# Decoder layer on one Trainium2 core: skip term and half of the causal convolution computed by TensorE with 32x32 diagonal blocks, and a new order of the side jobs

## The reference

```python
xn = norm_w * (x / rms)
xi, z = split(xn @ in_proj_w.T)                 # 1024 channels each
xc = silu(causal depthwise conv of 4 taps (xi) + conv_b)
dt, Bm, Cm = split(xc @ x_proj_w.T)             # 32, 16, 16
delta = softplus(dt @ dt_proj_w.T + dt_proj_b)
h[t] = exp(delta * A) * h[t-1] + delta * Bm * xc   # 1024 channels x 16 states
y = sum over states (h * Cm) + xc * Dp          # the last product is the skip term
out = x + (y * silu(z)) @ out_proj_w.T
```

## Time and profile before

| what | value |
|---|---|
| median of 3 runs | 2717.98 us (2713.64 to 2721.95) |
| the profiled execution: its time, its span | 2722.75 us, 2720.9 us |
| scan part (first to last scan) | 66.7 to 1973.2 us |
| steady stretch used below, 12 steps (rows 2 to 13) | 292.4 to 1745.8 us |
| experts | 2036 us to the end |

### The profile page before, as it was taken

One profiled execution on the slowest core, in us unless ns is written; L12 is line 12 of the kernel. 1 busy time (PEld: TensorE's weight loads), 2 busy tenths in 40 slices (PEclk: granted clock), 3 DMA queues, 4 the chain that ended last, 5 costly groups with the idle time before them and its releaser, 6 DMA issues.

```text
span 2720.9 us, 34850 instructions
## 1 busy us (share of the span) xinstructions
PE 2318.1 (85%) x12057; PEld 1902.7 (70%) x12057; DVE 2074.4 (76%) x2272; ACT 1779.4 (65%) x4075; POOL 1686.9 (62%) x996
## 2 busy tenths in 40 slices
PE   6778889888888888888888888887669999999997
PEld 6666666666666666766656666675539999999996
DVE  4999898899899899889999988988924454445443
ACT  5668787877778787877888887777743333333331
POOL 1988888889798888879798887979810100000100
PEclk9889998999899899989999998988879999999999
DMA  6050212212020211202020220202042432433320
GB/s 204 8 168 24 82 32 65 75 28 85 12 88 15 82 53 51 85 12 85 18 82 29 75 82 15 78 11 82 13 164 87 141 121 102 142 128 118 122 102 19
DMA packets 90876, 203.02 MB, mean 75 GB/s; under 512 B 7948, under 2 KB 16794, under 8 KB 90702
## 3 DMA queue, kind: packets, MB, share of 16 engines
q1 hardware_dynamic: 81486, 179.21, 20.3%
q0 software_dynamic: 5120, 14.21, 1.6%
q10 hardware_dynamic: 4096, 7.34, 0.9%
HBM read 171.32 MB, written 29.95 MB: 74 GB/s over the span
## 4 chain that ended last, share of the span: by engine, by line
PE 32%; DVE 30%; ACT 19%; issue 11%; POOL 5%; DMA 2%; SPq 0%; ACTq 0%; DVEq 0%; POOLq 0%
DVE ring L1267 15%; PE work L1633 12%; PE ring L1633 11%; ACT ring L831 9%; DVE arena L1276 5%; DVE arena L1110 4%; DVE arena L1267 3%; PE y L1613 3%; POOL arena L982 2%; PE work L1411 1%; POOL arena L987 1%; ACT arena L678 1%; DMA arena<-bc_rows 1%; ACT arena L553 1%; ACT arena L684 1%
## 5 line engine op out<-in xcount | busy, mean ns | idle before, releaser
L982 POOL TENSOR_TENSOR arena<-arena 128x896 f32<-128x896 f32 x512 | 1057.7, 2087 | 156.8 <-PE y L1613 148.4
L1267 DVE TENSOR_TENSOR_SCAN ring<-ring,arena 128x896 f32<-128x896 f32 x384 | 776.5, 2022 | 163.9 <-ACT ring L831 139.6
L831 ACT ACTIVATE ring<-arena,small 128x224 f32<-128x224 f32 x2048 | 793.6, 437 | 132.3 <-DVE arena L1276 124.2
L1613 PE MATMUL y<-cst_sb,arena 128*112 128x128 f32 x4096 | 556.5, 287 | 164.8 <-DVE arena L1276 124.2
L1613 PEld LDWEIGHTS y<-cst_sb,arena 128*112 128x112 f32 x4096 | 483.1, 140 | 255.0 <-DVE arena L1276 161.1
L1400 PE MATMUL work<-arena 128*128 128x224 f32 x2000 | 462.0, 389 | 36.5 <-DVE arena L1110 21.8
L1400 PEld LDWEIGHTS work<-arena 128*128 128x128 f32 x2000 | 415.2, 214 | 62.5 <-DVE arena L1110 26.3
L999 POOL DMA_INDIRECT out<-res,ids x32 | 44.7, 1395 | 642.0 <-DVE mst L1324 558.8
L1276 DVE TENSOR_TENSOR arena<-ring,arena 128x896 f32<-128x896 f32 x384 | 416.0, 1083 | 6.1 <-issue 0.2
L1339 DVE SCALAR_TENSOR_TENSOR hidden_lo<-work,hidden_hi 128x448 fp32r<-128x448 f32 x128 | 80.0, 625 | 344.9 <-ACT hidden_hi L881 344.9
L987 POOL TENSOR_TENSOR arena<-arena 128x896 f32<-128x896 f32 x128 | 266.6, 2083 | 96.8 <-DVE arena L1267 96.8
(11 more groups left out here) (210 smaller groups left out, 3352.0 us busy)
## 6 DMA issues: line engine op xcount, KB each, us to landing
weights<-in_w SPq DMA_DIRECT2D x64, 1024.0 KB, 7.2
arena<-bc_rows SPq DMA_DIRECT2D x128, 448.0 KB, 4.4
arena<-in_ctx SPq DMA_DIRECT2D x16, 896.0 KB, 5.8
expert_rows<-x2e SPq DMA_DIRECT2D x1, 7224.0 KB, 29.6
xrow<-expert_rows SPq DMA_DIRECT2D x8, 903.0 KB, 11.6
arena<-in_xT SPq DMA_DIRECT2D x16, 448.0 KB, 6.7
arena<-in_x SPq DMA_DIRECT2D x16, 448.0 KB, 3.6
out<-arena ACTq DMA_DIRECT2D x32, 224.0 KB, 2.3
```

What stands on the lines that cost most here:

```text
L831: last = nc.scalar.activation(decays[s % 2][:, i * L:(i + 1) * L], delta[:, k, :], ACT.Exp, scale=a_neg[:, n:n + 1])
L982: nc.gpsimd.tensor_tensor(u[:, u_of(b, s)], dx[:, k:k + 1, :].to_broadcast([P, QN, L]), bc[:, 0, q * QN:(q + 1) * QN, :], ALU.mult).then_i ...
L1267: nc.vector.tensor_tensor_scan(states, h, u_flat[:, u_of(b, s), :], 0.0, ALU.mult, ALU.add).then_inc(scan_done, 1)
L1613: last = nc.tensor.matmul(yt_bank[0:H, o:o + P], u[:, u_of(b, s), i, h * H:(h + 1) * H], ident, is_transpose=True, start=(s % (2 * Q) == 0 ...
```

## The change

- Two small tables of weights are made once at the start by POOL, 20 instructions of 32 partitions x 256 columns: `skip_w` and `taps_w` hold, for every 32 channels, a 32x32 diagonal block of Dp or of a convolution tap.
- The skip term is added by PE: `turn_back` issues per group four 32x32 matmuls (one per 32 channels, each on its own 32 partitions of input and output) ahead of the transposes. `skip_columns` is gone, and with it `y_bank`; the backs are now ordinary jobs of a work bank. There are three work banks in place of two (`job_bank` 0 to 2).
- The pairs 1 and 2 (`TURNED`) are convolved by PE: ACT copies the projection out in one instruction, PE does 2 groups x 4 taps x 4 blocks = 32 small matmuls in a job cv1 or cv2 (`convolve`), shifted by the tap, and ACT writes the result back with the bias (`convolved`, 2 instructions). DVE convolves pairs 0 and 3 as before.
- All due slots are new.

The diff, cut:

```diff
-        job_bank, h_bank, t_bank = wb + yb, wb, yb
+        job_bank, h_bank, t_bank = wb + [yb[1], yb[0]], wb, yb
...
-        PE_AT = {"xi0.0": 0, "xi0.1": 0.01, "xi1.0": 0.02, "xi1.1": 1, "xi2.0": 1.01, "xi2.1": 1.02, "tx0": 4, "tx1": 4.01,
-                 "rt": 4.02, "xi3.0": 4.03, "xi3.1": 4.04, "out0.0": 6, "out0.1": 7, "out0.2": 7.01, "out0.3": 7.02,
-                 "out1.0": 7.03, "out1.1": 7.04, "out1.2": 9, "out1.3": 9.01, "xp": 10, "dt0": 11, "t0": 12, "dt1": 14,
-                 "rank": 14.01, "z0.0": 15, "z0.1": 15.01, "z1.0": 15.02, "plug": 17, "z1.1": 20, "z2.0": 20.01,
-                 "z2.1": 20.02, "t1": 20.03, "dt2": 21, "z3.0": 23, "z3.1": 23.01, "dt3": 25, "ssq": 26, "xatt0.0": 27,
-                 "back0": 8.5, "back1": 16.5, "back2": 24.5, "back3": 0.5,
-                 "xatt0.1": 27.01, "xatt0.2": 27.02, "xatt1.0": 27.03, "xatt1.1": 32, "xatt1.2": 32.01}
+        PE_AT = {"xi0.0": 0, "xi0.1": 0.01, "xi1.0": 0.02, "xi1.1": 0.03, "back3": 0.04, "xi2.0": 3, "xi2.1": 3.01,
+                 "xi3.0": 3.02, "xi3.1": 3.03, "cv1": 3.04, "cv2": 7, "tx0": 10, "tx1": 10.01, "out0.0": 11, "out0.1": 11.01,
+                 "out0.2": 11.02, "out0.3": 11.03, "out1.0": 11.04, "out1.1": 11.05, "out1.2": 11.06, "out1.3": 11.07,
+                 "back0": 14, "xp": 15, "rt": 15.01, "dt0": 15.02, "dt1": 15.03, "z0.0": 19, "z0.1": 19.01, "z1.0": 19.02,
+                 "z1.1": 19.03, "back1": 19.04, "t0": 21, "plug": 23, "z2.0": 23.01, "z2.1": 23.02, "z3.0": 23.03, "z3.1": 23.04,
+                 "rank": 23.05, "dt2": 23.06, "dt3": 23.07, "back2": 25, "t1": 26, "xatt0.0": 26.01, "xatt0.1": 26.02,
+                 "ssq": 26.03, "xatt0.2": 26.04, "xatt1.0": 27, "xatt1.1": 27.01, "xatt1.2": 32}
-        ACT_AT = {"norm2.0": 1, "tap0": 3, "drop0": 3.01, "norm2.1": 4, "tap1": 4.01, "tap2": 4.02, "tx0": 5, "tx1": 5.01,
-                  "drop1": 6, "skip0": 6.01, "sq0": 7, "tap3": 8, "sq1": 9.01, "skip1": 14.01, "exp": 11, "silu": 11.01, "hx0": 12, "xp": 14,
-                  "skip2": 22, "sp0": 16, "t0": 16.5, "sp1": 18, "z0": 19, "depool": 21, "z1": 23, "hx1": 23.01, "z2": 24,
-                  "t1": 24.01, "sp2": 25.01, "skip3": 29, "z3": 27, "square": 27.01, "sp3": 28, "logs": 30, "yt0": 9, "yt1": 17, "yt2": 25, "yt3": 1.01}
+        ACT_AT = {"yt3": 1, "norm2.0": 2, "tap0": 3, "tap1": 3.01, "norm2.1": 4, "sq0": 4.01, "drop0": 6, "drop1": 6.01,
+                  "tap2": 7, "tap3": 7.01, "yt0": 10, "cv1": 11, "cv2": 11.01, "tx0": 12, "tx1": 12.01, "sq1": 14, "silu": 16,
+                  "hx0": 17, "xp": 19, "yt1": 19.01, "sp0": 20, "sp1": 20.01, "exp": 21, "z0": 23, "z1": 23.01, "hx1": 24,
+                  "t0": 24.01, "depool": 26, "yt2": 26.01, "z2": 27, "z3": 27.01, "square": 28, "sp2": 28.01, "sp3": 28.02,
+                  "t1": 29, "logs": 30}
...
+        DVE_AT = {"norm21.0": 1, "norm21.1": 1.01, "norm21.2": 1.02, "conv0.1": 4, "conv0.2": 4.01, "conv0.3": 4.02,
+                  "gate3": 4.03, "conv3.1": 7, "conv3.2": 7.01, "conv3.3": 7.02, "res0.0": 16, "res0.1": 16.01, "res0.2": 16.02,
+                  "res1.0": 16.03, "res1.1": 16.04, "res1.2": 16.05, "gate0": 17, "best.0": 20, "best.1": 20.01, "best.2": 20.02,
+                  "best.3": 20.03, "best.4": 20.04, "corr0": 20.05, "corr1": 20.06, "gate1": 23, "patches": 26, "chance.0": 27,
+                  "chance.1": 27.01, "slots.0": 27.02, "slots.1": 27.03, "slots.2": 27.04, "slots.3": 27.05, "corr2": 28,
+                  "corr3": 28.01, "gate2": 29, "w_xa": 29.01, "norm20.0": 30, "norm20.1": 30.01, "norm20.2": 30.02}
-        POOL_AT = {"delta1": 4, "delta2": 4.01, "delta3": 12, "scatter": 24, "ctx": 30, "delta0": 32, "xn": 32.01}
+        POOL_AT = {"delta1": 1, "delta2": 6, "delta3": 16, "ctx": 16.01, "scatter": 28, "delta0": 31, "xn": 31.01}
-        PE_FIRST = in_order("""xi0.0 xi0.1 xi1.0 xi1.1 xi2.0 xi2.1 xi3.0 xi3.1 counts z0.0 ...
+        PE_FIRST = in_order("""xi0.0 xi0.1 xi1.0 xi1.1 xi2.0 xi2.1 cv1 cv2 xi3.0 xi3.1 counts z0.0 ...
...
+            def convolved(b, par, j):
+                bank, free = job_full(act, b, f"cv{j}")
+                for i in range(2):
+                    k = 2 * j + i
+                    last = nc.scalar.activation(xc[:, 1 - par, k, :], bank[:, i * L:(i + 1) * L], ACT.Identity, bias=conv_b[:, k:k + 1])
+                last.then_inc(free, 1)
...
+            pool.wait_ge(s_small, 16)
+            pool.wait_ge(s_cst, 16)
+            for q in range(P // B):
+                rows = slice(q * B, (q + 1) * B)
+                one = ident[rows, rows].unsqueeze(1).to_broadcast([B, KB, B])
+                nc.gpsimd.tensor_tensor(skip_w[rows], one, d_skip[rows].unsqueeze(2).to_broadcast([B, KB, B]), ALU.mult).then_inc(diagonals, 1)
+                for tap in range(4):
+                    nc.gpsimd.tensor_tensor(taps_w[rows, :, tap, :], one, conv_w[rows, :, tap:tap + 1].to_broadcast([B, KB, B]),
+                                            ALU.mult).then_inc(diagonals, 1)
...
+            def turn_back(step, scanned, j):
+                bank, full = start_job(step, f"back{j}")
                 for i in range(2):
+                    k = 2 * j + i
+                    for q in range(P // B):
+                        rows = slice(q * B, (q + 1) * B)
+                        nc.tensor.matmul(bank[rows, i * L:(i + 1) * L], skip_w[rows, k, :], xc[rows, scanned % 2, k, :], start=True, stop=False,
+                                         skip_group_check=True)
+                    if i == 0:
+                        pe.wait_ge(yt_copied, scanned * PAIRS + (j + 1))
                     for h in range(2):
...
+            def convolve(b, par, j):
+                bank, full = start_job(b, f"cv{j}")
+                job_copied(pe, b, f"xi{j}")
+                for i in range(2):
+                    k = 2 * j + i
+                    for back in range(4):
+                        for q in range(P // B):
+                            rows = slice(q * B, (q + 1) * B)
+                            last = nc.tensor.matmul(bank[rows, i * L + back:(i + 1) * L], taps_w[rows, k, 3 - back, :],
+                                                    xc[rows, 1 - par, k, 0:L - back], start=(back == 0), stop=(back == 3), skip_group_check=True)
+                last.then_inc(full, 1)
```

More of the change, by code:

```diff
@@ L46, in build_decoder @@
     UB = 5
+    B = 32
+    TURNED = (1, 2)
+    BY_DVE = tuple(j for j in range(PAIRS) if j not in TURNED)
+    LEFT = len(BY_DVE)
     u_of = lambda b, s: (b * SLOTS + s) % UB
@@ L281, in build_decoder @@
-        DVE_AT = {"norm21.0": 1, "norm21.1": 1.01, "norm21.2": 2, "conv0.1": 3, "conv0.2": 3.01, "conv0.3": 3.02,
[7 rows of a table removed]
-        POOL_AT = {"delta1": 4, "delta2": 4.01, "delta3": 12, "scatter": 24, "ctx": 30, "delta0": 32, "xn": 32.01}
+        JOB_BANK = {"cv1": 1, "cv2": 2, "xi0": 0, "xi1": 2, "xi2": 2, "xi3": 0, "tx0": 0, "tx1": 1, "rt": 2, "rank": 2, "xp": 0,
+                    "out0": 2, "out1": 0, "dt0": 1, "dt1": 0, "dt2": 0, "dt3": 1, "z0": 2, "z1": 0, "z2": 1, "z3": 0, "t0": 1,
+                    "t1": 0, "plug": 2, "ssq": 2, "xatt0": 1, "xatt1": 2, "back0": 2, "back1": 2, "back2": 2, "back3": 1}
@@ L293, in build_decoder @@
-        ACT_FIRST = in_order("""w_z tap0 tap1 tap2 tap3 silu z0 square xp sp0 sp1 sp2 sp3 z1 logs z2 z3""")
-        DVE_FIRST = in_order("""conv0.1 conv0.2 conv0.3 conv1.1 conv1.2 conv1.3 conv2.1 conv2.2 conv2.3 conv3.1
+        PE_FIRST = in_order("""xi0.0 xi0.1 xi1.0 xi1.1 xi2.0 xi2.1 cv1 cv2 xi3.0 xi3.1 counts z0.0 z0.1 xp dt0 dt1 dt2 dt3 ssq z1.0 z1.1 z2.0
+                               z2.1 z3.0 z3.1""")
+        ACT_FIRST = in_order("""w_z tap0 tap1 tap2 cv1 cv2 tap3 silu z0 square xp sp0 sp1 sp2 sp3 z1 logs z2 z3""")
@@ L295, in build_decoder @@
+        DVE_FIRST = in_order("""conv0.1 conv0.2 conv0.3 conv3.1
                                 conv3.2 conv3.3 counted corr0 corr1 corr2 corr3""")
@@ L679, in gates @@
                 if pro:
-                    jobs_copied(act, b, ("xi0", "xi1", "xi2", "xi3"))
+                    jobs_copied(act, b, tuple(f"cv{j}" if j in TURNED else f"xi{j}" for j in range(PAIRS)))
                     apart(act)
-                    act.wait_ge(conv_done, (b + 1) * 4 + 4)
+                    need(act, conv_done, (b + 2) * LEFT)
                     apart(act)
```

113 lines of the change are left out of this document (58 added, 55 removed), and 8 rows, old and new, of tables (AHEAD, DVE_AT).

## The result

The changed kernel takes **2635.8 us** (median of four runs, 2632.2 to 2643.1) where the kernel before takes 2719.9 (2713.6 to 2722.0, four runs): ratio 0.970, 95% interval 0.967 to 0.973. The forecast was 2675 (2600 to 2750), rival 1 had said 2627. The profiled execution took 2643.05 us with a span of 2641.2, so 79.7 less than the 2720.9 of before.

| stretch | before | after | difference | forecast |
|---|---|---|---|---|
| start to first scan | 66.7 | 84.3 | +17.6 | +16 |
| first to last scan | 1904.5 | 1807.4 | -97.1 | -59 |
| last scan to end | 749.7 | 749.5 | -0.2 | 0 |
| a steady step (mean of 12) | 121.1 | 113.9 | -7.2 | -3.9 |
| of it DVE busy | 108.5 | 105.1 | -3.4 | -4.3 |

A forecast was written before the change was run, and what follows sets the result against it. DVE was taken to set the step. Fourteen steps at -3.9 us (-55), step 0 at -4.3, step 15 at 0 and the start at +16 made -43, so 2675 us against the median 2717.98; range 2600 to 2750.

The forecast's parts named there:

- rival 1: PE's small blocks overlap almost fully, 0.05 us per record; idle time 10, step 114.2, total 2627 us; chance 0.23.
- The small record: PE's 192 small-matmul records per step in convolution and skip term: 0.10 us each by half overlap, 19 us per step.
- rival 2: PE becomes the bound: no overlap, 0.19 us per record, step 130.5, total 2878 us; chance 0.17.
- The idle time at slot 16: DVE waits 6.4 us for u of slot 16, behind PE's output projection of 13.7 us at slot 11.
- the 13 us: DVE's total idle time per step in the new order, summed over its slots, giving a step of 117.2 us.
- Slot 8: DVE idle some 1.5 us there, after PE's 13.4 us of transposes, projections and cv1 at slot 3.
- Slot 17 behind delta3 and ctx: POOL's delta3 and ctx after u 16 delay u 17 by 5.8 us, leaving DVE 2 us idle.
- ACT and PE in slots 27 to 31: About 12 us of side work on ACT, as before, leaving 2 us idle; 1 us more for small latencies.
- sign of failure, idle below 9: The forecast is wrong if DVE's idle time per step is below 9 or above 16 us.
- DVE's work: DVE loses 12 tap instructions of 0.36 us per step: -4.3 us, from 108.5 to 104.2.
- The clock: PE's granted clock, 0.92 in the steps, costs some 10 us per step; denser work should hold 2.4 GHz.
- The start: Before the first scan: POOL's blocks start the projection 4 us later, the convolution chain adds 12.5; together +16 us.

The follow-up runs named there:

- e3: Changed kernel with pair 2 convolved by DVE again (six DVE taps more, cv2 less): 2669.0 us, ratio 0.981 to the kernel before.
- e1: Changed kernel with the loops of convolve exchanged, so the four taps of one 32x32 block follow each other: 2656.5 us, ratio 0.977 to the kernel before.
- e6: Changed kernel with the skip term as one full 128x128 diagonal matmul per group, tap weights for turned groups only: 2624.6 us, ratio 0.964 to the kernel before.
- e12: Changed kernel with only four of the five buffers of u used: 2905.1 us, ratio 1.069 to the kernel before.
- e4: Changed kernel with POOL's 20 block instructions moved behind its first normalisation: 2626.0 us, ratio 0.965 to the kernel before.
- e10: Changed kernel with POOL's blocks behind the first normalised rows and one full diagonal skip matmul per group: 2617.6 us, ratio 0.961 to the kernel before.
- e2: Changed kernel's new operations in the due slots of the kernel before, cv1 and cv2 close behind the projections: 2852.3 us, ratio 1.049 to the kernel before.
- e8: New operations in the old order, with ACT's copies of cv1 and cv2 due later and cv2 at PE 8: 2826.9 us, ratio 1.038 to the kernel before.
- e5: Changed kernel with POOL's scatter of the routed rows moved from slot 28 to the end of slot 31: 2654.1 us, ratio 0.975 to the kernel before.

## Why the prediction came out as it did

The time lies in its range, 39 us below the forecast, and the sign is right. The mechanism was the one named: DVE sets the step (e3), the new PE work fits beside it, and the start pays. Rival 1 is nearer than the forecast in step (114.2 for 113.9), idle time (10 for 8.8) and total (2627). The sum was too high in two terms, the price of a small record and the idle time, and right in a third, the start, by luck:

- **The small record.** Taken 0.10 us, "about half overlap"; it is 0.049 in the convolution and 0.064 in the skip term. PE's new work is 128 x 0.049 + 64 x 0.064 = 10.4 us per step, where 19 were reckoned. Of the reason given one half is right: the two passes of one block do start 0.19 us apart. The other is wrong: not only the block before runs beside them, but all four do, so eight records take two such pitches and four take 0.196 us, where one full record takes 0.19. The "against" of rival 2, disjoint rows and columns, is what e1 shows: the queue order alone is worth a factor 2.3. The sum also left out a price for changing between small and full records, 0.09 us each way (e6). The Trainium skill ("TensorEngine Tiling (Array Packing)", restrictions) says that different row tiles can't access one PSUM bank at once, by which nothing would have overlapped; here they did, each block on its own 32 partitions of that bank: this trace doesn't agree. The Trainium skill's page "PSUM — Partial Sum Buffer" (PSUM bank collisions raise a hardware error) quotes the same rule for two writes of TensorE, but what it reports as measured is an error for row tiles in one bank and one quadrant of 32 partitions; this case has one block per quadrant, which doesn't contradict that.
- **It mattered less than it seems.** e1 puts 8 us of it back and the step grows by half a microsecond. The idle time didn't hang on the price of a record, up to at least 0.11 in the cv jobs. The prediction's "about 0.13" for PE as the bound was not reached by any run; at 0.11 PE is busy 97.6%.
- **The idle time at slot 16: the step that failed.** "u of slot 16 is there after 17.5 us: 6.4 us idle" took PE's condition one slot too strict. The line is `need(pool, sum_done, b * SLOTS + s - UB + 1)`: the *count* s - 4 is reached when the slots 0 to s - 5 are turned. (The sentence in the description of the kernel before, and the prediction's, that slot s needs slot s-4, is a misreading of mine; it is s - 5, in both kernels.) So slot 16 is free before the piece starts, and slot 17 has DVE's residual work of slot 16 as cover as well. Measured: nothing before the scan of slot 16, 0.4 us before that of slot 17. e12 makes the condition what I took it for, and the 6.66 us appear. It was the largest single item of the 13 us.
- **The other idle items.** Slot 8: 1.5 predicted, 0 measured. Either of two things is enough for that: e1 has none with 0.11 per record and five buffers, e12 none with cheap records and four. Dear records and four buffers together were not run. Slot 17 behind delta3 and ctx: 2 predicted, 0.3 measured (same misreading, a slot more of cover; with four buffers, in e12, it is 1.7). ACT and PE in slots 27 to 31: 2 predicted, 2.4 measured (0.9 before the corrections of slot 28, 1.5 around slot 30). Not predicted: 2.0 at the change of step and 1.1 before slot 2, mostly behind POOL's delta0, xn and delta1; 0.6 before slot 7; 0.6 before gate1 at slot 23. Sum with what is too small to list: 8.8. The forecast's own sign of failure, idle below 9, is met by a hair.
- **DVE's work.** -4.3 predicted, -3.4 measured (union of busy time; 12 taps per step are gone). The groups of taps shrink by 4.8 us per step when each instruction is summed; some of that was overlap with neighbours. I haven't traced the remaining 0.9.
- **The clock.** The forecast named it, without a number in its sum. It is 0.97 in the steps after, 0.92 before; before, most of the steps took 119.2 or 123.1, with PE at 0.50 in the earlier trace rows behind eight us (672.8 to 680.8) in which it was busy for 4.3, and after they lie between 113.1 and 115.9. How much of the gain hangs on the clock no run separates.
- **The start: +16 forecast, +17.6 measured, for other reasons.** POOL was to delay the projection by 4 us and delayed it by 11.4: the blocks took 20 us, not 14 (DVE held POOL up for some 8 us of it, see the last section), and stood in front of the rows. The convolution's chain was to cost 12.5 and cost 6.3, again by the price of the record (two cv jobs in 6.2 us, not 12.8). Two errors of 6 to 7 us cancelled. e4 and e10 show the first to be nearly all avoidable.
- **The new order.** The prediction treated it as a source of waits. e2 and e8 show that the operations need it: in the old order they lose 104 us and more. DVE's waits for ACT's decays, 9.6 us per step before, are 1.6 after; which of the new due slots does that isn't shown.

## What to carry over

When a wait is on a counter, write down which index reaches it before you count slots of cover: one off in a ring of five was 6 us per step on paper, and 17 us per step in e12. Small matmuls on disjoint 32x32 blocks are worth their order in the queue: issue neighbours on different blocks, and change between small and full records as seldom as you can. A job that one engine does early or waits in may cost nothing where it stands (e5); before it is moved, look at who is latest at the new place, and put one-time set-up work behind the first instruction that others wait for (e4).

## What the runs showed of the hardware

- With 224 moving columns, fp32: four 32x32 diagonal blocks of one bank, issued in turn, 0.049 us per record; the same blocks issued one block at a time 0.11; a full 128x128 record 0.19 in both kernels. The records of one block start 0.19 us apart in both orders. So four blocks cost what one full matmul costs, and a full diagonal is no dearer than four blocks: in e6 it is cheaper (0.38 us for a group against 0.51), by 0.09 us for each change between small and full.
- POOL and DVE hold each other up for whole instructions, and it depends on what DVE runs. Rows of the start of after, of DVE and then of POOL:

```profile
12.69 2.10 DVE L1067 TENSOR_TENSOR digits<-arena 112x1568 fp32r<-112x1568 f32 x1
14.71 2.73 DVE L1086 TENSOR_SCALAR arena<-arena,small 128x1024 f32<-128x1024 f32 x4
17.36 1.77 DVE L1071 TENSOR_REDUCE arena<-arena 112x112 f32<-112x1568 f32 x1
...
19.47 2.09 DVE L1075 TENSOR_TENSOR digits<-arena,cst_sb 112x1792 fp32r<-112x1792 f32 x1
```

```profile
19.64 2.40 POOL L923 TENSOR_TENSOR taps_w<-cst_sb,small 32x256 f32<-32x256 f32 x1
22.12 0.61 POOL L921 TENSOR_TENSOR skip_w<-cst_sb,small 32x256 f32<-32x256 f32 x1
```

  One block instruction of POOL takes 0.61 us when DVE is quiet (22.12). The one begun at 13.21, of 4.70 us, starts inside a TENSOR_TENSOR of DVE with both inputs in SBUF, lasts through the four TENSOR_SCALAR of the weight table behind it, and ends 0.47 us after the last of them. The one begun at 19.64, of 2.40 us, starts inside another such TENSOR_TENSOR and ends 0.48 us after it. The blocks beside TENSOR_REDUCE, from 17.88 on, take their usual 0.62. It goes the other way too: in the kernel before, the same four TENSOR_SCALAR took 4.56 us, where POOL's normalisation of the earlier trace rows (15.47 to 17.6) fell into them, and that normalisation takes 3.21 and 3.02 us in e4 and e10, 2.07 in after with DVE quiet. The Trainium skill ("SBUF — State Buffer", SBUF: two separate sides) names a port pair that DVE and GpSimd take in turn, for whole instructions, when DVE runs in a two-port mode or reads two SBUF inputs. These rows agree with it. So do the steady steps, where POOL's u keeps its 2.09 us beside DVE's scans and products (105 us of DVE and 102 us of POOL in steps of 114): each of these reads one of its two inputs from `ring`, which is in PSUM.
- Twenty such blocks cost POOL 20.3 us in after, 13.8 in e4, and the 16 smaller with one full table 10.0 in e10. A block instruction of half the columns (128 in place of 256) took 0.50 us for 0.59: at this size the cost is mostly fixed.
